# Two-stage cross-attention: seven block products for two of the products, one-pass scores, a bias folded by TensorE

## What is computed

```python
q = einsum('blh,oh->blo', x, w_q); k = einsum('bsh,oh->bso', c, w_k); v = einsum('bsh,oh->bso', c, w_v)
probs = softmax(einsum('blh,bsh->bls', q, k) / sqrt(512), axis=-1)
x = x + alpha * einsum('blh,oh->blo', einsum('bls,bsh->blh', probs, v), w_o)
g_x = conv1x1(g_w, g_b, c).T; theta_x = conv1x1(theta_w, theta_b, x).T; phi_x = conv1x1(phi_w, phi_b, c)
y = einsum('bnm,bmc->bnc', einsum('bnc,bcm->bnm', theta_x, phi_x) / 512, g_x).T
wy = conv1x1(w_w, w_b, y)
out = bn_gamma * (wy - bn_mean) * rsqrt(bn_var + 1e-5) + bn_beta + x
```

## Time and profile before

| what | us |
|---|---|
| median of 3 runs | 388.59 (388.55 to 388.94) |
| span of the profiled execution | 386.3 |
| TensorE busy | 381.0 |
| VectorE busy | 310.8 |
| ScalarE busy | 205.4 |
| GpSimd busy | 3.7 |
| HBM read and written | 51.32 MB and 18.89 MB |

### The profile page before, as it was taken

The page is one execution under the profiler, slowest core; times in us unless marked ns, Lnnn a source line. Parts: engine busy times, 40 slices in busy tenths (PEclk is TensorE's granted clock), DMA queues, the critical chain, the costliest instruction groups (busy, mean ns, idle before and its releaser), DMA issues.

```text
span 386.3 us, 5597 instructions
## 1 busy us (share of the span) xinstructions
PE 381.0 (99%) x1776; PEld 318.6 (82%) x1776; DVE 310.8 (80%) x595; ACT 205.4 (53%) x441; POOL 3.7 (1%) x7
## 2 busy tenths in 40 slices
PE   8999999999999999999999999999999999999995
PEld 5888878888888888888888888888888888888885
DVE  4999779987599776996689866996779875996786
ACT  3477568533664267543665257452665346552553
POOL 0001000000000000000000000000000000000000
PEclk9999999999999999999999999999999999999999
DMA  8995842486375646556383556565375564043423
GB/s 242 382 331 188 285 133 54 158 296 225 116 256 145 238 141 211 182 171 217 109 271 112 214 170 198 189 198 188 123 219 181 191 190 136 15 121 144 151 87 110
DMA packets 58059, 70.37 MB, mean 182 GB/s; under 512 B 5056, under 2 KB 47936, under 8 KB 54976
## 3 DMA queue, kind: packets, MB, share of 16 engines
q1 hardware_dynamic: 56144, 67.21, 53.2%
q10 hardware_dynamic: 1904, 3.02, 2.5%
HBM read 51.32 MB, written 18.89 MB: 182 GB/s over the span
## 4 chain that ended last, share of the span: by engine, by line
PE 97%; DMA 1%; DVE 1%; ACT 0%; issue 0%; SPq 0%
PE bank L367 23%; PE bank L368 23%; PE bank L369 23%; PE bank L421 8%; PE bank L440 7%; PE bank L407 5%; PE bank L429 4%; PE bank L462 2%; PE bank L466 1%; DMA xb<-w_k 1%; DVE xb L1143 0%; DVE xb L1138 0%; PE bank L393 0%; ACT theta_hi L621 0%; ACT t_sides L621 0%
## 5 line engine op out<-in xcount | busy, mean ns | idle before, releaser
L367 PE MATMUL bank<-ov_hi,c_sides 128*128 128x512 f32 x128 | 50.0, 391 | 0.0
L368 PE MATMUL bank<-c_sides,qk_hi 128*128 128x512 f32 x128 | 49.9, 390 | 0.0
L369 PE MATMUL bank<-c_sides,qk_lo 128*128 128x512 f32 x128 | 49.9, 390 | 0.0
L368 PE MATMUL bank<-ov_lo,c_sides 128*128 128x512 f32 x128 | 49.9, 390 | 0.0
L367 PE MATMUL bank<-c_sides,qk_hi 128*128 128x512 f32 x128 | 49.8, 389 | 0.0
L369 PE MATMUL bank<-ov_hi,c_sides 128*128 128x512 f32 x128 | 49.8, 389 | 0.0
L621 ACT ACTIVATE t_sides<-bank 128x512 fp32r<-128x512 f32 x32 | 19.0, 594 | 37.2 <-PE bank L369 37.2
L421 PE MATMUL bank<-t_sides,xT_hi 128*128 128x512 f32 x128 | 31.9, 391 | 0.0
L877 DVE TENSOR_TENSOR vo_lo<-bank,vo_hi 128x512 fp32r<-128x512 f32 x32 | 21.8, 685 | 11.8 <-ACT vo_hi L621 10.9
L621 ACT ACTIVATE probs<-bank 128x512 f32<-128x512 f32 x16 | 9.4, 585 | 37.9 <-PE bank L429 37.9
L367 PEld LDWEIGHTS bank<-ov_hi,c_sides 128*128 128x128 f32 x128 | 24.1, 188 | 5.2 <-DVE wg_sides L877 0.4
(11 more groups left out here) (148 smaller groups left out, 820.9 us busy)
## 6 DMA issues: line engine op xcount, KB each, us to landing
cT_raw<-ctx_t SPq DMA_DIRECT2D x8, 1024.0 KB, 4.8
xT_raw<-x_t SPq DMA_DIRECT2D x8, 1024.0 KB, 5.1
c_raw<-ctx_n SPq DMA_DIRECT2D x8, 1024.0 KB, 6.5
xb<-x SPq DMA_DIRECT2D x16, 512.0 KB, 4.2
out<-xb SPq DMA_DIRECT2D x14, 512.0 KB, 2.8
gram_moved<-gram_blocks SPq DMA_DIRECT2D x16, 256.0 KB, 2.3
gram_blocks<-gram_moved SPq DMA_DIRECT2D x64, 64.0 KB, 2.0
moved<-blocks SPq DMA_DIRECT2D x16, 256.0 KB, 2.3
```

The source lines that it names most:

```text
L367: pe.matmul(dst, ahi, bhi, start=(k == 0), stop=False)
L368: pe.matmul(dst, ahi, blo, start=False, stop=False)
L369: mm = pe.matmul(dst, alo, bhi, start=False, stop=(k == k_tiles - 1))
```

## The change

1. The products tT and vo are made by seven block products instead of eight (Winograd's form of Strassen's scheme) over 2 x 2 blocks: qk and ov are cut in blocks of 256 x 256, stored as `[P, 7, 2, 256]` with four sum blocks (S1, N2, S3, S4); of the context four mixed blocks `mix` are made in each pair. Each block product is twelve matmuls of 256 columns (`half_product`). Results are put together in PSUM: a chain bank that is copied by ScalarE into a seed bank (`copy_chain`), a join bank whose content ScalarE keeps in SBUF (`keep_join`), and VectorE's `join` and `join_side`, with TensorE waiting for each.
2. GpSimd makes the four mixed blocks (`mix_sum`) and their low parts (`mix_part`) in every pair, in the buffer of c after its sums; two of the first pair's low parts are VectorE's.
3. Scores are made in one pass of three 256-column matmuls a tile into one bank; the copy of low scores and the sum are gone, maximum and exponential read PSUM. `w_g_phi` likewise: t1 is one operation a batch.
4. g_b is folded by TensorE (a third product in `combine_w_g`), GpSimd's reduction is gone; the batch norm's scale is computed per column, sent to DRAM and fetched as a row.
5. The casts of w_o go from VectorE to ScalarE, the square root goes among the weights, loads on SP are reordered, c's sums of the next pair are made at the pair's start (with a copy of the sums in `sums_now`), x1 shares vo's buffer, theta shares pT's, banks are dealt anew, and the first pair has an order of its own on ScalarE and VectorE (`first_order`).

The diff, cut to its core:

```diff
+            def context(i, kt):
+
+                if i in MIXED_SIDE:
+                    return cut(mix, every, MIXED_SIDE[i], kt)
+                k, b = {M1: (kt, 0), M2: (2 + kt, 0), M3: (2 + kt, 1)}[i]
+                return cut(cT, every, k, b)
+
+            def half_product(dst, lhsT, rhs, opens):
+
+                for n in range(2):
+                    for kt in range(2):
+                        (ahi, alo), (bhi, blo) = lhsT(n, kt), rhs(n, kt)
+                        at = dst[:, n * S:(n + 1) * S]
+                        pe.matmul(at, ahi, bhi, start=(opens and n == 0 and kt == 0), stop=False, skip_group_check=True)
+                        pe.matmul(at, ahi, blo, start=False, stop=False, skip_group_check=True)
+                        mm = pe.matmul(at, alo, bhi, start=False, stop=(kt == 1), skip_group_check=True)
+                return mm
...
+            def t_product(i, to_bank, opens=False):
+
+                half_product(bank[to_bank], lambda n, kt: cut(qk, every, i, kt, tile(n)),
+                             lambda n, kt: context(i, kt), opens).then_inc(tT_done, 1)
+
+            def v_product(i, to_bank, opens=False):
+
+                half_product(bank[to_bank], lambda n, kt: [t[:, tile(n)] for t in context(i, kt)],
+                             lambda n, kt: cut(ov, every, i, kt), opens).then_inc(vo_done, 1)
...
+                scores(0)
                 pe.wait_ge(xT_lo, two[2])
+                scores(1)
                 if not first:
                     pe.wait_ge(out_made, four[-2])
-                high_scores(0, range(KH - 1))
-                pe.wait_ge(tT_lo, four[4])
-                high_scores(0, [KH - 1])
-                if not first:
-                    pe.wait_ge(out_made, four[0])
-                high_scores(1, [0])
-                low_scores(0, stop=True).then_inc(scores_done, 1)
-                low_scores(1)
-                high_scores(1, range(1, KH), stop=True).then_inc(scores_done, 1)
+                v_product(M1, VO_CHAIN, opens=True)
+                if first:
+                    pe.wait_ge(gram_read, 1)
+                    pe.wait_ge(ov_sum_lo, 2)
+                else:
+                    pe.wait_ge(phi_turned, p + 1)
+                v_product(M5, VO_JOIN, opens=True)
...
+                v_product(M2, VO_SEED)
+                pe.wait_ge(vo_joined, two[1])
+                v_product(M7, VO_CHAIN)
+                v_product(M3, VO_JOIN)
+                pe.wait_ge(vo_joined, two[2])
+                v_product(M4, VO_CHAIN)
...
-                    values(1, st)
+                    w_g_phi([0] if last else [0, 1])
...
+                if not first:
+                    pe.wait_ge(x1_made, four[2])
+                    t_product(M1, TT_CHAIN, opens=True)
+                    pe.wait_ge(mix_lo, four[5])
+                    t_product(M5, TT_JOIN, opens=True)
+                    pe.wait_ge(x1_made, four[4])
+                    theta_rows(0, [four[1], four[2]])
+                pe.wait_ge(tT_copied, two[3])
+                pe.wait_ge(mix_lo, four[6])
+                t_product(M6, TT_CHAIN)
...
+                pe.wait_ge(tT_joined, two[3])
+                pe.wait_ge(mix_lo, four[7])
+                t_product(M7, TT_CHAIN)
...
+                t_product(M3, TT_JOIN)
+                pe.wait_ge(tT_joined, two[4])
+                pe.wait_ge(mix_lo, four[8])
+                t_product(M4, TT_CHAIN)
...
+            def copy_chain(to_bank, from_bank, done, count, copied):
+                act.wait_ge(done, count)
+                act.activation(bank[to_bank][:], bank[from_bank][:], ACT.Identity).then_inc(copied, 1)
+
+            def keep_join(side, from_bank, done, count, copied):
+                act.wait_ge(done, count)
+                act.activation(side, bank[from_bank][:].rearrange("p (n s) -> p n s", n=2), ACT.Identity).then_inc(copied, 1)
...
+                if not last:
+                    c_sums(loads[16], kept=p)
+                v_sums()
+                if not last:
+                    xT_part(0, loads[32])
...
+                copy_chain(VO_SEED, VO_CHAIN, vo_done, seven[1], vo_copied)
...
+                keep_join(vo_side, VO_JOIN, vo_done, seven[2], vo_copied)
+                u_part()
+                if not last:
+                    cT_part(0, loads[32], seven[1])
                 pT_part(0)
+                vo_part(0, HALF[0], VO_SEED, seven[4])
+                vo_side_part()
+                vo_part(1, HALF[0], VO_JOIN, seven[6])
+                vo_part(0, HALF[1], VO_CHAIN, seven[7])
+                pT_part(1)
...
+            def join(side, join_bank, chain_bank, done, count, kept, copied, joined):
+                dve.wait_ge(copied, kept)
+                dve.wait_ge(done, count)
+                dve.tensor_tensor(bank[join_bank][:], bank[chain_bank][:], side.rearrange("p n s -> p (n s)"),
+                                  ALU.add).then_inc(joined, 1)
+
+            def join_side(side, chain_bank, done, count, joined):
+                dve.wait_ge(done, count)
+                dve.tensor_tensor(side, in_halves(chain_bank), side, ALU.add).then_inc(joined, 1)
...
                 def row_maxima(b):
-                    dve.wait_ge(low_scores_copied, two[b + 1])
-                    dve.tensor_tensor(probs[:, b], banks[:, SCORE_BANK[b], 0:S], probs[:, b],
-                                      ALU.add).then_inc(scores_summed, 1)
-                    dve.wait_ge(scores_summed, two[b + 1])
-                    dve.tensor_reduce(row_max[:, b], probs[:, b], AX.X, ALU.max).then_inc(max_made, 1)
+                    dve.wait_ge(scores_done, two[b + 1])
+                    dve.tensor_reduce(row_max[:, b], bank[SCORE_BANK[b]][:].rearrange("p (t s) -> p t s", t=KL), AX.X,
+                                      ALU.max).then_inc(max_made, 1)
...
+                if not last:
+                    xT_part(0, two[3])
+                join(vo_side, VO_JOIN, VO_CHAIN, vo_done, seven[3], two[2], vo_copied, vo_joined)
+                u_rows()
+                if not last:
+                    xT_part(1, two[4])
+                join_side(vo_side, VO_CHAIN, vo_done, seven[5], vo_joined)
+                u_part()
+                if not last:
+                    cT_part(0, two[3])
+                vo_part(0, HALF[0], in_halves(VO_SEED), four[1])
+                pT_part(0)
+                vo_part(0, HALF[1], in_halves(VO_CHAIN), four[4])
+                vo_part(1, HALF[1], vo_side, four[2])
+                vo_part(1, HALF[0], in_halves(VO_JOIN), four[3])
+                pT_part(1)
...
+            def mix_sum(n, one, other, op):
+                pool.tensor_tensor(mix_raw[:, n], one, other, op).then_inc(mix_made, 1)
+
+            def mix_part(n, count):
+                pool.wait_ge(mix_hi, count)
+                pool.tensor_tensor(mix[1][:, n], mix_raw[:, n], mix[0][:, n].bitcast(F32), ALU.subtract).then_inc(mix_lo, 1)
+
+            def mixes(made, sides_loaded, shared=False):
+                pool.wait_ge(cT_loaded, sides_loaded)
+                mix_sum(T1, C12, C11, ALU.subtract)
+                pool.wait_ge(mix_made, made[1])
+                mix_sum(N2C, mix_raw[:, T1], C22, ALU.subtract)
+                mix_sum(T3, C22, C12, ALU.subtract)
+                pool.wait_ge(mix_made, made[2])
+                mix_sum(N4C, mix_raw[:, N2C], C21, ALU.add)
+                if not shared:
+                    mix_part(T1, made[1])
+                    mix_part(N2C, made[2])
+                else:
+                    pool.wait_ge(mix_lo, made[2])
+                mix_part(T3, made[3])
+                mix_part(N4C, made[4])
+
+            pool.wait_ge(w_lo, 4 * KH)
+            mixes(range(5), 16, shared=True)
+            for n, which in enumerate((S3, S1, N2, S4)):
+                pool.wait_ge(ov_hi, 4 + n)
...
+            def pair(p):
+                loads, four = counts(pool, p, 16, [32]), counts(pool, p, 4, range(5, 9))
+                pool.wait_ge(c_summed, four[8])
+                mixes([None] + [four[n] for n in range(5, 9)], loads[32])
```

More of the change, by code:

```diff
@@ L606, in pair @@
                 pe.wait_ge(t1_lo, two[2])
-                pe.wait_ge(theta_lo, two[2])
-                pe.wait_ge(tT_lo, four[6])
                 for ct in range(KL):
@@ L740, in x1_part @@
                 def x1_part(b, lt):
-                    if lt == 0 and not first:
-                        act.wait_ge(theta_done, two[-1 + b])
+                    act.wait_ge(delta_done, four[2 * b + 2])
                     act.wait_ge(x1_made, four[2 * b + lt + 1])
@@ L1185, in pair @@
-                for half in range(2):
-                    cT_part(half, two[3 + half])
-                    if first and half == 0:
-                        u_part()
+                t1_rows([0, 1])
+                turn_sums(four[8], stores[16 * BLOCKS])
+                keep_sums(four[4])
                 x1_rows(0)
-                if first:
-                    turn_sums(8, 16 * BLOCKS)
```

(3 more changed lines are left out.)

1014 lines of the change are left out of this document (595 added, 419 removed).

## The result

Before 388.57 us (388.42 to 388.94), after 405.74 us (three of four runs from 405.63 to 405.82, one 409.96): a ratio of 1.0467, 95% interval 1.0421 to 1.0512. 384.5 us was forecast. The profiled execution has a span of 404.1 us, 1.6 less than its run.

The account below looks back on a forecast made before the run. TensorE was taken to bound the kernel: 88.3 us to pair 1, 260.4 for six loop pairs of 43.4 and 33.5 for the last made a span of 382.2, with 2.3 more a run of 384.5 us; range 378 to 392.

Parts of the forecast that it names:

- What bounds it, TensorE's sum: Loop pair: only TensorE time counts; its products sum to 42.95 us after the change, 44.21 before.
- 120 ns in long runs: TensorE: 256-column products start 120 ns apart, also in runs of over 100; bounds 113 and 122 ns.
- the rival of dear products: Short products cost 124 ns in long runs, a pair 0.9 us longer, 391.9 us as a run; chance 0.10.
- M6's cover of 0.07 us: Values: ScalarE's copy of M1's bank ends at 8.57 us, M6 is due at 8.64; 0.1 us added.
- delta(0): Loop pair: TensorE waits 0.35 us for M4's low part; in the last pair it waits 1.0 us.
- Second half: tT's joins come ... each is early by 0.5 us or more: Loop pair: tT's joins come while TensorE has theta, output or another block product to do, so no wait.
- the same prices: Step times from the rows: product to next engine 0.28 us, ScalarE copy 0.60, VectorE's result 0.69.
- GpSimd: size: Eight 128x512 operations with two inputs a pair take 1.3 to 1.6 us each; up to 4.2 us costs nothing.
- VectorE is held by GpSimd: Rival: weighted sums wait for GpSimd, TensorE waits 0.7 to 1 us a pair; 392.1 us as a run; chance 0.12.
- Prologue and first pair: Pair 1 could start at 85.6 us; waits of 2.7 us (bounds 1 and 4.5) make it 88.3, against 87.75 before.
- Last pair: Scores +0.2, values -0.8, delta(0) waits 1.0 us: 33.5 us against 33.1 before.
- no cost, and none of the other way round either: Queues: on SP the load of c moves behind both gram fetches, with xT's load and the stores behind it, at no cost.

Follow-up runs that it names:

- e2: The changed kernel with GpSimd's four sums of the mixed blocks cut to 4 of every 256 columns in the loop's pairs: 405.38 us.
- e11: The changed kernel with x1's parts of batch 1 earlier in the second half, the weighting of the sums and v's sums later in the first: 391.50 us.
- e1: The changed kernel with GpSimd's four low parts of the mixed blocks cut to 4 of every 256 columns in the loop's pairs: 398.61 us.
- e14: e11 with ScalarE, not VectorE, scaling the row maxima (128x2): 391.23 us.
- e13: The changed kernel with e11's first half alone (weighting of the sums and v's sums later), second half as it was: 409.70 us.
- e16: e11 with GpSimd's four sums cut to 4 of every 256 columns in the loop's pairs: 391.28 us.

## Why the prediction was wrong

- *What bounds it, TensorE's sum: right.* 42.95 us forecast, 42.94 measured. *120 ns in long runs: right*, so the rival of dear products falls.
- *Values, first half.* M6's cover of 0.07 us was given 0.1 us; it waited 0.46 in loop pair 3 and 1.73 in pair 1. delta(0): 0.35 forecast, 0.27 measured. The prediction's own steps give 17.54 - 17.28 = 0.26; the 0.35 that went into the sum does not follow from them.
- *"Second half: tT's joins come ... each is early by 0.5 us or more": this step failed.* Both were late, by 1.17 and 1.20 us, 2.4 of the 3.0 us a pair that the forecast missed. It took "the same prices" from steps at which GpSimd stands still, and it followed the products alone and not VectorE's queue, in which x1's low parts stand ahead of both joins, and gram squares, their DMA and their closing ahead of the side join.
- *GpSimd: size right, cost wrong.* 1.30 to 1.57 us each, as taken; but they cost 3.9 us of VectorE in a pair. Four x1 low parts take 0.62 us more each, two weighted sums 0.5, two negated maxima 0.22: 2.5 + 1.0 + 0.4, against the 3.7 between VectorE's 40.5 and the forecast 36.8.
- *The rival "VectorE is held by GpSimd" was the true one, at 0.12.* Its place was wrong: it stood on the weighted sums (e2: 0.4 us in all) and named x1's low parts in half a sentence, without following what is late behind them. So its 44.3 us a pair became 46.4, and the kernel lay outside the range by 13.7 us. It was priced down by one row, a VectorE operation of 0.69 us at 18.75 inside a GpSimd one. That GpSimd operation had one input and half the columns, and still took 1.60 us where one of 128x512 takes 1.30 alone, so it may itself have been waiting. Two rows speak for that, one of the kernel before and one of e11:

```profile
18.14 0.69 DVE L877 TENSOR_TENSOR xT_lo<-c_raw,xT_hi 128x512 fp32r<-128x512 f32 x1
...
44.72 0.75 POOL L1534 TENSOR_TENSOR phi_blocks<-phi_blocks,rows_moved 128x256 f32<-128x256 f32 x1
```

GpSimd's operation of 18.57 was issued inside VectorE's of 18.14, and a GpSimd operation of 128x256, with two inputs even, takes 0.75 us. From its end, 20.17, back by 0.75 us is 19.42, and VectorE's second low part ended at 19.44. By this estimate GpSimd had waited for both, so the row quoted against the rival is more likely a case of it. The rule of the Trainium skill, "SBUF — State Buffer", section "Who interferes with whom", was cited for it. For VectorE's steps with two SBUF inputs the traces agree: 1307 ns beside GpSimd's low parts and 749 where they are cut short (e1), while steps that read PSUM were untouched. The step of 128x2 has one SBUF input, which the rule as cited doesn't cover; it was held as well, to the end of GpSimd's sum. The rule should have outweighed one ambiguous row.
- *Prologue and first pair: base right, waits mis-sized.* Pair 1 started at 90.85 instead of 88.3. Without waits it would be 85.05 (85.6 forecast); the waits are 2.26 in the prologue and 3.55 in the first pair, 5.8 against 2.7 taken, beyond the upper bound of 4.5. TensorE was held 1.1 us by the low parts of c; GpSimd's sums beside them account for 0.9 (3.26 us for two instead of 2.36).
- *Last pair* 34.7 instead of 33.5: 0.95 ahead of delta(0) as forecast (1.0), and 0.8 around theta that it hadn't.
- *Queues, "no cost, and none of the other way round either": not followed far enough.* The gram's fetch, 4.4 us later in the pair, came to lie beside the sums' fetch, and its pieces took 2.2 to 3.7 us instead of 2.0 in pair 3. The moved load of c was not seen to cost anything in the changed kernel itself; in e1 the last piece took 4.9 to 5.9 us with it close behind and 3.5 us without.

Together: 2.55 (start) + 18.1 (loop) + 1.2 (end) - 0.7 (a run is 1.6 above its span, not 2.3) = 21.2 us.

## What to carry to other kernels

When work goes to an idle engine, list each operation of its neighbour that lies beside it and has both inputs in SBUF (here a small step with one was held too), and price those at the sum of both, before pricing the new work at nothing; then follow the neighbour's queue, step by step, to the last transfer and join behind it, and look what other transfers are issued at the new time of that one. A change that makes one engine leaner by 3% leaves that much less cover for everyone else: nearly the same work in other orders took 389.7 to 409.7 us here, so the order is part of the change. An edit that removes a wait is judged by the kernel's time and the next waits in the list, not by that wait.

## What the runs showed that I had not expected

In one execution TensorE's clock fell behind a wait. In e14's profiled execution it stood still from 131.1 to 133.03 us, ahead of a late side join, and then the clock was at the lower level (window, length, busy times, and after them the granted clock, 1.00 being the 2.4 GHz level and 0.50 the 1.2 GHz level):

```profile
131.00:133.00 2.00, 0.23 (x2) 0.02 (x1) 1.47 (x4) 0.67 (x2) 0.00 (x0) 1.00 1.00 422
133.00:136.00 3.00, 2.97 (x13) 2.98 (x14) 3.00 (x6) 1.13 (x3) 0.00 (x0) 0.52 0.50 210
136.00:137.00 1.00, 1.00 (x4) 0.73 (x4) 1.00 (x3) 1.00 (x3) 0.00 (x0) 0.73 0.71 291
137.00:140.00 3.00, 3.00 (x19) 2.67 (x18) 2.35 (x4) 1.98 (x8) 0.85 (x1) 1.00 0.40 140
```

The starts of the 256-column products after it lay 213 ns apart instead of 120, and the wait of 1.96 us cost 1.7 us more. In e13 waits of 1.6 to 2.8 us at the same place in six pairs were followed by products at 120 ns, so not each such wait is followed by it; that the wait was the cause is likely, not shown, and what decides wasn't tried.

And a VectorE step of two elements a partition can take 1.18 us instead of 0.17, for no reason of its own: with GpSimd's sums cut short (e16) it took 0.17.
